# Second-stage weights made inside the last state-space chunk, and the last output projection split

## What is computed

```python
x = x + _L0_attn_ref(_layernorm(x), in_proj_w, conv_w, conv_b, x_proj_w, dt_proj_w, dt_proj_b, out_proj_w, A_log, D_param)
x = x + _L0_ffn_ref(_layernorm(x), factors, bias)
x = x + _L1_attn_ref(_layernorm(x), Wq, Wk, Wv, Wo, rms_w)
x = x + _L1_ffn_ref(_layernorm(x), ...)
```

## Time and profile before

| | us |
|---|---|
| median of 3 runs | 5323.17 (5321.68 to 5325.96) |
| the profiled execution's own time | 5325.68 |
| its span | 5323.8 |
| first stage, to the barrier | 0 to 3724.9 |
| second stage: set-up, to the first statistics | 3724.9 to 3793.5 |
| second stage: 64 tiles | 3793.5 to about 5200 |
| busy: PE, DVE, ACT, POOL | 4817.2 (90%), 4447.0 (84%), 2689.8 (51%), 3155.8 (59%) |

### The profile page before, as it was taken

One profiled execution on the slowest core, in us unless ns is written; L12 is line 12 of the kernel. 1 busy time (PEld: TensorE's weight loads), 2 busy tenths in 40 slices (PEclk: granted clock), 3 DMA queues, 4 the chain that ended last, 5 costly groups with the idle time before them and its releaser, 6 DMA issues. The chain is left out here.

```text
span 5323.8 us, 108656 instructions
## 1 busy us (share of the span) xinstructions
PE 4817.2 (90%) x44199; PEld 2788.8 (52%) x44199; DVE 4447.0 (84%) x7289; ACT 2689.8 (51%) x4364; POOL 3155.8 (59%) x1639
## 2 busy tenths in 40 slices
PE   6899999999999999999999999987499999999973
PEld 3344444444444444444444444433388888888862
DVE  3989889898998989889898898985578888888876
ACT  3666666666666666666566665652133333333320
POOL 1676776767767676676766767675144443444436
PEclk9999999999999999999999999998699999999995
DMA  2222212222222222222222222221300000000003
GB/s 86 84 92 85 97 72 104 94 82 104 73 104 89 88 102 75 97 89 87 101 82 96 86 90 102 75 96 64 129 26 28 26 28 26 28 28 26 28 22 78
DMA packets 117198, 394.68 MB, mean 74 GB/s; under 512 B 26720, under 2 KB 28384, under 8 KB 83808
## 3 DMA queue, kind: packets, MB, share of 16 engines
q1 hardware_dynamic: 107040, 383.95, 20.5%
q0 software_dynamic: 6336, 0.18, 0.3%
q10 hardware_dynamic: 3328, 3.61, 0.2%
HBM read 348.20 MB, written 39.50 MB: 73 GB/s over the span
## 5 line engine op out<-in xcount | busy, mean ns | idle before, releaser
L336 POOL TENSOR_TENSOR s<-s,Cb 128x1024 f32<-128x1024 f32 x1024 | 2394.1, 2359 | 996.2 <-DVE state L654 991.9
L649 DVE TENSOR_TENSOR_SCAN s<-s,state,BU 128x512 f32<-128x512 f32 x2048 | 2453.2, 1260 | 368.2 <-PE BU L738 347.7
L505 ACT ACTIVATE s<-dt,ch 128x512 f32<-128x512 f32 x2048 | 1307.0, 715 | 718.9 <-PE Y L755 717.4
L755 PE MATMUL Y<-s,ident 64*64 64x512 f32 x8192 | 1010.4, 609 | 67.0 <-POOL s L336 66.7
L681 PE MATMUL PJ<-xnT,w_in 128*128 128x512 f32 x2048 | 947.0, 606 | 30.1 <-ACT xnT L372 15.3
L738 PEld LDWEIGHTS BU<-spread,dtuT 32*128 32x128 f32 x16384 | 512.3, 189 | 529.7 <-DVE s L649 338.3
L738 PE MATMUL BU<-spread,dtuT 32*128 32x128 f32 x16384 | 609.9, 286 | 146.4 <-DVE s L649 145.7
L681 PEld LDWEIGHTS PJ<-xnT,w_in 128*128 128x128 f32 x2048 | 369.9, 190 | 502.7 <-issue 423.8
L755 PEld LDWEIGHTS Y<-s,ident 64*64 64x64 f32 x8192 | 277.6, 134 | 563.6 <-issue 527.7
L729 PE MATMUL PJ<-w_out,u 128*128 128x512 f32 x1024 | 471.3, 604 | 7.9 <-ACT xnT L372 6.4
L1105 POOL TENSOR_TENSOR x1t<-x1t,bias_b 128x512 f32<-128x512 f32 x64 | 83.0, 1296 | 398.9 <-DVE xa L1291 398.9
(11 more groups left out here) (223 smaller groups left out, 6951.4 us busy)
## 6 DMA issues: line engine op xcount, KB each, us to landing
Cb<-bc SPq DMA_DIRECT2D x256, 1024.0 KB, 4.8
res<-in_x SPq DMA_DIRECT2D x64, 256.0 KB, 5.0
x<-res SPq DMA_DIRECT2D x64, 256.0 KB, 5.1
x1t<-x SPq DMA_DIRECT2D x64, 256.0 KB, 2.6
out<-r_t SPq DMA_DIRECT2D x64, 256.0 KB, 2.0
xt<-in_x SPq DMA_DIRECT2D x31, 512.0 KB, 5.7
rows_of<-out SPq DMA_DIRECT2D x10, 512.0 KB, 7.5
out<-rows_of SPq DMA_DIRECT2D x10, 512.0 KB, 3.6
```

The lines of the kernel that those rows point to most:

```text
L336: nc.gpsimd.tensor_tensor(pair, pair, Cb[q % 2][:, 2 * part * T:2 * part * T + 2 * T], ALU.mult).then_inc(z_ready, 1)
L505: nc.scalar.activation(s[k % SLOTS][:, n, :], dt[p % 2][:, gi, :], ACT.Exp, scale=ch[:, 2 * p + gi, 7 + 4 * nq + n:8 + 4 * nq + n]).then_i ...
L649: nc.vector.tensor_tensor_scan(s[k % SLOTS][:, n, :], s[k % SLOTS][:, n, :], BU[:, n::4], state[:, b, k, n:n + 1], ALU.mult, ALU.add).then ...
L755: last_ = nc.tensor.matmul(Y[r][y_rows(r, gi), :], ident[rows, rows], s[(k_even + gi) % SLOTS][rows, n, :], start=False, stop=(n == 3 and ...
```

## The change

Into the last chunk of the first stage (`last` is its flag) go:

- SP loads the 8 factors and Wq, Wk, Wv, Wo into tiles that this chunk no longer needs (`w_in`, `xnT`, the other slot of `u`), waits for the parts made of them and stores these, ten of 1 MB, in a DRAM tensor `w_parts`.
- DVE adds the factors, in 14 halves of 128x1024 (`ADD_AT`), and makes the low part of their sum (`FACTOR_LOW_AT`).
- ACT makes the high parts (`NEXT_HIGH_AT`) and scales Wo.
- POOL makes the low parts of q, k, v, o, in 16 instructions of 128x512 (`NEXT_LOW_AT`).
- PE does six of eight out_proj groups of output tiles 0 and 1 at k = 26 to 31 (`LAST_OUT_AT`), those of tile 2 after the last scan and those of tile 3 after the last sum; tiles 2 and 3 use banks of BU. After the last `y_out` eight matmuls are left. The residual's four tiles are loaded at k = 14.

The second stage then only loads. POOL issues the ten loads from `w_parts`, f first, the others once the tables that DVE needs first are there; POOL's own loop starts after them. SP and ACT issue the tables in another order, nine of them only after the first tokens. DVE waits for six tables before it starts, for the others at its second tile; each product waits for its own weights. `rms_w` is loaded in the first stage, as a fourth small load of ACT's queue that `small_loaded` waits for. Some semaphores are merged.

```diff
+        ADD_AT = {7: (1, 0), 8: (1, 1), 10: (2, 0), 11: (2, 1), 12: (3, 0), 14: (3, 1), 15: (4, 0), 16: (4, 1),
+                  18: (5, 0), 19: (5, 1), 20: (6, 0), 21: (6, 1), 23: (7, 0), 24: (7, 1)}
+        FACTOR_AT = {9: 3, 12: 4, 15: 5, 17: 6, 20: 7}
+        FACTOR_LOW_AT = {27: 0, 28: 1}
+        NEXT_LOAD_AT = {5: 0, 13: 1, 15: 2, 23: 3}
+        NEXT_HIGH_AT = {6: 0, 14: 1, 17: 2, 24: 3, 25: 4}
+        NEXT_LOW_AT = {k: (i, kb) for i, k0 in enumerate((8, 16, 20, 26)) for kb, k in enumerate(range(k0, k0 + KB))}
+        NEXT_STORE_AT = {13: 0, 21: 1, 25: 2, 31: 3, 30: 4}
+        LAST_OUT_AT = {26 + i: (i // 3, i % 3) for i in range(6)}
...
+                    if last and k in NEXT_LOW_AT:
+                        i, kb = NEXT_LOW_AT[k]
+                        raw = next_raw[i % 2][:, kb * T:(kb + 1) * T]
+                        pool.wait_ge(high_made, i + 1)
+                        nc.gpsimd.tensor_tensor(raw.bitcast(F32R), raw, next_high[i % 2][:, kb * T:(kb + 1) * T],
+                                                ALU.subtract).then_inc(low_made, 1)
...
-            act.wait_ge(small_loaded, 48)
+            act.dma_start(rms_scale[:], next_w["rms_w"]).then_inc(small_loaded, 16)
+            act.wait_ge(small_loaded, 64)
...
+                        if last and k - 1 in NEXT_HIGH_AT:
+                            next_high_part(k - 1)
...
                 def piece(k):
 
+                    if last and k in ADD_AT:
+                        add_factor(*ADD_AT[k])
+                    if last and k in FACTOR_LOW_AT:
+                        factor_low(FACTOR_LOW_AT[k])
...
+                    if last and k in LAST_OUT_AT:
+                        j, q = LAST_OUT_AT[k]
+                        if k == 26:
+                            pe.wait_ge(y_ready, c * G + 6)
+                        for g in (2 * q, 2 * q + 1):
+                            nc.tensor.matmul(last_bank(j), u[1][:, g, j * P:(j + 1) * P], w_out[:, g, :],
+                                             start=(g == 0), stop=False)
...
+            pe.wait_ge(scan_done, 4 * NCH * U)
+            last_early(2)
             for part in range(2):
                 pe.wait_ge(z_ready, NCH * 2 * U - 1 + part)
+                pe.sem_inc(steps, 1)
                 y_sum(U - 2, part)
+            last_early(3)
             pe.wait_ge(y_ready, G * NCH)
...
+            load_parts(4, "f", "f_loaded")
+            pool.wait_ge(S["tab_loaded"], 16 * 6)
+            for i, n, loaded in ((0, "q", "qk_loaded"), (1, "k", "qk_loaded"), (2, "v", "vo_loaded"), (3, "o", "vo_loaded")):
+                load_parts(i, n, loaded)
+            pool.wait_ge(S["w_loaded2"], 16 * 13)
```

More of the change, by code:

```diff
@@ L167, in mamba_block @@
                       + uses("tr0", *two) + uses("gate", 5), "steady")
-        after = ring(uses("out", *range(NT)), "after")
+        out_full = sem("out_full")
         GATE_AT = {3: 6, 4: 7, 21: 0, 22: 1, 26: 2, 27: 3, 30: 4, 31: 5}
@@ L208, in held @@
                 wait(sp, sem_, value)
[L209 removed]
+                sp.sem_inc(steps, 1)
             for cols, loaded in ((slice(0, INTER), w_hid_loaded), (slice(INTER, 2 * INTER), w_loaded)):
@@ L282, in body @@
                         store_bc(steady, c, 1 - b)
+                    if last:
+                        prepare(k, c)
+                        if k == 14:
+                            for j in range(NT):
+                                if j < 2:
+                                    held(x1_stored[j], 16 * 2 * (NCH - 1))
+                                else:
+                                    held(res_loaded[j - 2], 16 * (2 * (NCH - 1) + 1))
+                                sp.dma_start(last_res(j), x_v[1, NI - 1, :, j, :]).then_inc(res_loaded[j % 2], 16)
             periods(sp, body)
@@ L476, in late, with next_high_part @@
                         square(steady, k - 24, c)
+                def next_high_part(k):
+                    i = NEXT_HIGH_AT[k]
+                    if i == len(NEXT):
+                        act.wait_ge(factor_added, 2 * (RANKS - 1))
+                        nc.scalar.copy(factor[1].bitcast(F32R), factor_sum).then_inc(high_made, 1)
+                        return
+                    raw = next_raw[i % 2]
+                    act.wait_ge(next_loaded, 16 * (i + 1))
+                    if NEXT[i] == "o":
+                        for kb in range(KB):
+                            rows = raw[:, kb * T:(kb + 1) * T]
+                            nc.scalar.activation(rows, rows, ACT.Copy, scale=rms_scale[:, kb:kb + 1])
+                        act.drain()
+                    nc.scalar.copy(next_high[i % 2].bitcast(F32R), raw).then_inc(high_made, 1)
                 def early(k):
@@ L866, in _, with last_early, blocks_after @@
             periods(pe, body)
+            def last_early(j):
+                for g in range(6):
+                    nc.tensor.matmul(last_bank(j), u[1][:, g, j * P:(j + 1) * P], w_out[:, g, :],
+                                     start=(g == 0), stop=False)
+            pe.wait_ge(scan_done, 4 * NCH * U)
+            last_early(2)
             for part in range(2):
                 pe.wait_ge(z_ready, NCH * 2 * U - 1 + part)
+                pe.sem_inc(steps, 1)
                 y_sum(U - 2, part)
+            last_early(3)
             pe.wait_ge(y_ready, G * NCH)
             for j in range(NT):
-                if j >= 2:
-                    pe.wait_ge(after.taken["dve"], j - 1)
-                for part in range(2):
-                    last_ = out_proj(PJ[after.bank(("out", j))], j, part, 1)
-                last_.then_inc(after.full, 1)
-def blocks_after(nc, x1, w, out):
+                for g in range(6, G):
+                    last_ = nc.tensor.matmul(last_bank(j), u[1][:, g, j * P:(j + 1) * P], w_out[:, g, :],
+                                             start=False, stop=(g == G - 1))
+                last_.then_inc(out_full, 1)
+def blocks_after(nc, x1, w_parts, w, out):
     BATCH, SEQ, HID = x1.shape
@@ L1078, in body @@
                     sp.dma_start(rot[s_][:], w["rot"][i]).then_inc(rot_loaded[s_], 16)
+                    if num(a) == 0:
+                        for dst, src in late:
+                            sp.dma_start(dst[:], src).then_inc(S["w_loaded2"], 16)
                 a = back(t, 6)
```

199 lines of the change are left out of this document (123 added, 76 removed).

## The result

The changed kernel takes **5293.18 us** in the median of 5 runs (5292.37 to 5294.45), the kernel before 5323.17 in the same runs: a ratio of 0.994, 95% interval 0.9927 to 0.9953. So it is faster, as forecast, but by 30.0 us (0.56%) and not by 54.8, and the time lies 3 us above the range, 24.8 above the forecast of 5268.4. The profiled execution took 5292.37, span 5290.5, 33.3 us less than the span of before. So 21.5 of the 24.8 us lie inside the trace. The other 3.3 lie between execution and median: I had taken 2.5 us off for the median, and the median came out 0.8 above the profiled execution.

A forecast was written before the change was run, and what follows sets the result against it. DVE's scans (4.80 us) and wait for BU (1.10) set a plain step; the set-up waits for loads and DVE. Sum +1.0 - 16.6 - 54.2 + 15 = -54.8 from 5325.7, less 2.5: 5268 us, range 5250 to 5290.

The forecast's parts named there:

- Leaves ... the 64 tiles alone: Second stage's tiles: the change does not touch them, so no time was counted for them.
- Set-up, -54.2: Second stage's set-up: first root at B + 12.4 instead of B + 69.6, saving 57.2 us, less 3 us of waits.
- B + 7.0: Set-up: DVE's first instruction, 7.0 us after the second stage's start B, 4.2 us after the last needed table's issue.
- rival 2: Set-up: the weights or POOL's issues are late, +12 to +31 us, 5280 to 5299; chance 0.13.
- Last chunk, +15: First stage's last chunk: DVE's adds collide with POOL's low parts 13.5, late sums 2.5, adds alone 0.5, gain -1.7 us.
- ACT's and PE's additions lie in their idle time. I count nothing: Last chunk: work added to ACT and PE fits their idle time, ACT's reaching 10.76 us; nothing counted.
- Tail, -16.6: First stage's end: early out_proj matmuls end out_proj at 21.3 us after the last scan, not 38.2; bounds 14 and 17.5.
- Start, +1.0: Kernel's start: a fourth small load behind `mask` on ACT's queue delays all that follows, 0.3 to 1.4 us, taken as 1.0.
- Rivals 1: Last chunk: adds and low parts don't collide, chunk +3 us instead of +15, 5256; chance 0.16.
- 3: Last chunk: late sums at the slow pace feed back in each step, +15 us more, 5283; chance 0.09.
- 4: Tail: early out_proj only moves PE's work, half of the tail's gain is lost, 5276; chance 0.04.
- 5: Last chunk: SP's queue makes Cb loads late and POOL waits, slower than before; 8 us late each gives 5372; chance 0.02.

The follow-up runs named there:

- pad16: The changed kernel with 16 unused bytes put behind the weights in the place of `rms_w`: 5280.6 us, ratio 0.9918 to the kernel before.
- before_shift: The kernel before the change, with only 16 unused bytes (32 with alignment) added behind `rms_w`: 5335.9 us beside 5324.1, ratio 1.0023.
- ftab: The changed kernel with waits at first use, late tables issued after x1 of tile 2, f's loads issued once six small loads landed: 5285.5 us.
- no_early: The changed kernel with all 32 out_proj matmuls of the last chunk after `y_out`, as before the change: 5311.1 us, 17.9 more than the change.

## Why the prediction was wrong, by its own steps

- **"Leaves ... the 64 tiles alone"** is the step that failed and that no rival covered: +12.3 us, 57% of the 21.5 by which the sum was off. I looked at what instructions the tiles have, and not at where their operands lie. `pad16` and `before_shift` show the cause from both sides. That the products of f, q, k and v are slower where weights and activations lie apart modulo 64 fits all eighteen traces; what in the chip makes it so, and why the product with Wo doesn't show it, stays open.
- **Set-up, -54.2:** measured -41.2. Two of its entries failed. "B + 7.0" for the tables took the landing time of a queue that had the engines to itself; f's 2 MB beside it made it 12.05 (+5.0; `ftab` shows 5.4 without them). "I count nothing" for DVE's second tile was worked out from bytes and rate: 5.5 MB by B + 15. But the last small tables shared the engines with q to o and landed at B + 35.7, and DVE stood 14.8 us. The rate itself was right (387 to 416 GB/s from 3730 to 3754). POOL's issues were a third of what I had taken, so of the two entries of rival 2 that one fell and the other, late loads, came true by way of the tables, not the weights. The measured 5293 lies in that rival's 5280 to 5299; as to the kernel's time that is luck, since its price of 12 to 31 us stands for the set-up alone, which missed by 13.0, and the tiles' 12.3 came on top while the chunk gave 5.7 back.
- **Last chunk, +15:** measured +9.3. The pair of its largest entry was right (adds and low parts together: 5 to 6 us, gone with either partner; the lock shows in the rows) and its size was not, 13.5 and 2.5 forecast. The lag of POOL did not stay from step to step: only some steps grew, by 1.8 to 2.5 us, and others got it back. And "ACT's and PE's additions lie in their idle time. I count nothing" missed 3.7 us: ACT's idle time in the whole is no cover for one wait for a load that stands ahead of the copies that BU needs. The -1.7 for the early out_proj isn't shown (`no_early`).
- **Tail, -16.6:** right, -17.0, by the steps of its working. **Start, +1.0:** +1.4 here, but 0.1 to 1.6 in the traces of the other kernels that load `rms_scale` there, so that it came so near is in part luck. The kernel's first scan shows the load more clearly: at 117.6 to 119.5 us in the 14 traces that have it at the start, at 116.3 to 116.9 in the four others.
- Rivals 1 (chunk +3), 3, 4 and 5 did not come true; the out_proj parts did in the tail what they say (`no_early`), and POOL never waited for Cb.

## What to carry to other kernels

When a change removes or adds a tile in SBUF, compare the addresses of everything behind it, the operands of the matmuls first, even if their instructions are untouched. Put a wait for a load at the first use of what it loads, with a semaphore for each thing that is waited for, and keep small tables off the engines while megabytes move on another queue, or ahead of them. An engine's idle share covers an added instruction only if nothing urgent is queued behind the wait that this instruction brings.

## What was unexpected of the hardware

- The products with f, q, k and v, with moving operands of 128x512, follow one another faster when weights and transposed activations lie at the same place modulo 64 bytes than when they lie 32 apart: every 0.229 us against 0.233 in the v product, at a granted clock of 1.00 in both. The product with Wo runs at 0.233 in both placements.
- The lock costs the second comer nearly the rest of the first one's time in both directions: 1.27 became 2.26 on POOL under an add of 1.26, and 1.20 became 2.29 on DVE under a low part of 1.27.
- With loads on two queues the engines reached more than the 399 GB/s that I had taken as the rate, in the set-up of the changed kernel:

```profile
3742.00:3746.00 4.00, 2.99 (x8) 1.86 (x6) 0.00 (x0) 0.00 (x0) 0.00 (x0) 0.65 1.13 413
3746.00:3750.00 4.00, 0.00 (x0) 0.00 (x0) 0.00 (x0) 0.00 (x0) 0.00 (x0) 0.77 1.37 416
```

The 358 GB/s of the Trainium skill (DMA: Bandwidth & Descriptors, Where 436 GB/s comes from), a stack's 716 divided by two cores, are exceeded there by 16% with one core running; the measurement decides.
